# Moving the transposes of the attention probabilities one head closer to their scores, in both attentions of a decoder layer

## The reference, cut to what matters

```
def attention(q, k, v, mask):               # 16 heads of 32 channels
    scores = einsum('bhqd,bhkd->bhqk', q, k) / sqrt(32)
    scores = scores * mask - 10000.0 * (1.0 - mask)
    probs = softmax(scores, axis=-1)
    return einsum('bhqk,bhkd->bhqd', probs, v)
ln_out = layernorm(hidden_states, ln1_s, ln1_b)
q, k, v = split(ln_out @ w_qkv + b_qkv, 3)
x = hidden_states + merge_heads(attention(q, k, v, ltor_mask)) @ w_ao + b_ao
ln_out = layernorm(x, ln2_s, ln2_b)
q = ln_out @ w_q + b_q;  k, v = split(encoder_states @ w_kv + b_kv, 2)
x = x + merge_heads(attention(q, k, v, cross_mask)) @ w_co + b_co
```

## Time and profile before

| | us |
|---|---|
| time, median of 3 runs (4130.07 to 4134.7) | 4130.2 |
| time of the profiled execution | 4134.31 |
| its span | 4132.5 |
| PE busy / DVE busy / ACT busy / POOL busy | 3711.9 / 2993.9 / 2051.7 / 1781.3 |
| first and last L599 of the attentions, from the span's start | 31.1 and 1493.2 |

### The profile page before, as it was taken

How to read it: one execution, slowest core, us unless ns; L and a number is a source line. 1 busy time by engine, 2 the same in 40 slices (tenths; PEclk the granted TensorE clock), 3 DMA queues, 4 the chain that set the end, 5 groups by cost and what they waited for, 6 DMA issues and landing times. The chain is left out here.

```text
span 4132.5 us, 71545 instructions
## 1 busy us (share of the span) xinstructions
PE 3711.9 (90%) x21636; PEld 2875.0 (70%) x21636; DVE 2993.9 (72%) x6732; ACT 2051.7 (50%) x5384; POOL 1781.3 (43%) x1257
## 2 busy tenths in 40 slices
PE   7999999999999969999999679999999999999976
PEld 6777777777777848999999446666666666666633
DVE  6777778888888855665565178888887877888872
ACT  5777777777777755555555213333333333333322
POOL 5444445644444420000000146666566666666652
PEclk9999999999999979999999879999999999999987
DMA  5344344544444441000100300000000000000000
GB/s 147 98 115 107 91 107 115 147 107 118 129 122 111 117 124 52 30 30 31 46 30 26 115 18 14 24 25 24 24 24 25 24 24 24 20 24 18 22 18 15
DMA packets 146675, 256.58 MB, mean 62 GB/s; under 512 B 27248, under 2 KB 32112, under 8 KB 145488
## 3 DMA queue, kind: packets, MB, share of 16 engines
q1 hardware_dynamic: 146512, 254.50, 22.3%
HBM read 107.62 MB, written 33.55 MB: 34 GB/s over the span
## 5 line engine op out<-in xcount | busy, mean ns | idle before, releaser
L432 POOL TENSOR_TENSOR a_prob<-a_prob,a_rsums 128x512 f32<-128x512 f32 x512 | 540.4, 1057 | 780.6 <-DVE a_rsums L610 780.4
L1310 POOL TENSOR_TENSOR c_S<-c_S,c_rT 128x1024 f32<-128x1024 f32 x256 | 558.1, 2180 | 466.4 <-DVE c_S L1588 426.4
L1588 DVE TENSOR_TENSOR_SCAN c_S<-c_wT,c_s,c_vb 128x256 f32<-128x256 f32 x1024 | 709.1, 734 | 46.5 <-issue 4.9
L504 ACT ACTIVATE a_prob<-a_t,a_tmin 128x256 f32<-128x256 f32 x1024 | 512.7, 501 | 366.4 <-DVE a_tmin L603 365.2
L1583 DVE TENSOR_TENSOR c_vb<-c_kT,c_vb 128x512 f32<-128x512 f32 x512 | 352.5, 688 | 293.9 <-PE c_vb L1754 262.2
L599 DVE SCALAR_TENSOR_TENSOR a_ps_s<-a_ps_s,a_mask 128x512 f32<-128x512 f32 x512 | 357.4, 698 | 179.7 <-PE a_ps_s L700 110.6
L603 DVE CUSTOM_DVE_ANT_0 a_t<-a_ps_s,a_mneg 128x256 f32<-128x256 f32 x1024 | 394.2, 422 | 60.1 <-issue 0.7
L1754 PE MATMUL c_vb<-c_vhl,c_spread 128*128 128x512 f32 x512 | 300.7, 597 | 74.5 <-DVE c_S L1588 61.9
L710 PE MATMUL a_ps_t<-w_ident,a_prob 128*128 128x128 f32 x2048 | 323.7, 282 | 27.8 <-ACT a_probT L514 18.1
L971 PE MATMUL b_ps<-b_ln_high,b_w_high 128*128 128x256 f32 x1024 | 291.1, 284 | 15.9 <-DVE b_ln_low L913 15.9
L700 PE MATMUL a_ps_s<-a_stack 96*128 96x256 f32 x1024 | 230.4, 307 | 81.6 <-DMA a_stack<-a_parts_qk 64.6
(11 more groups left out here) (219 smaller groups left out, 9570.6 us busy)
## 6 DMA issues: line engine op xcount, KB each, us to landing
a_stack<-a_parts_qk SPq DMA_DIRECT2D x768, 128.0 KB, 2.4
x<-a_xb SPq DMA_DIRECT2D x32, 512.0 KB, 2.8
a_x_in<-in_x SPq DMA_DIRECT2D x16, 512.0 KB, 3.6
a_xb<-in_x SPq DMA_DIRECT2D x16, 512.0 KB, 3.5
a_x_in<-x SPq DMA_DIRECT2D x16, 512.0 KB, 3.7
a_enc<-in_ctx SPq DMA_DIRECT2D x16, 512.0 KB, 4.4
a_xb<-x SPq DMA_DIRECT2D x16, 512.0 KB, 3.6
b_x_in<-x SPq DMA_DIRECT2D x16, 512.0 KB, 5.1
```

Of the source, the lines that this page charges most:

```text
L432: nc.gpsimd.tensor_tensor(prob[:, h % 4, :, :], prob[:, h % 4, :, :], rsums[:, h, :].unsqueeze(2).to_broadcast([P, TC, T]), ALU.mult).then ...
L504: op = nc.scalar.activation(prob[:, n % 4, tc, :], t[:, n % 2, tc, :], ACT.Exp, bias=tmin[:, n, tc:tc + 1], scale=-1.0, accum_out=psums[:, ...
L1310: nc.gpsimd.tensor_tensor(S[:, n % 4, :, 0:T], S[:, n % 4, :, 0:T], rT[:, par, :, :], ALU.mult).then_inc(z_ready, 1)
L1588: op = nc.vector.tensor_tensor_scan(S[:, n % 4, c, 1:T + 1], wT[:, par, c, :], vb[:, c, :], s0[:, par, c, n:n + 1], ALU.mult, ALU.add)
```

## The change

`LT` becomes 2. With it the transposes of head h stand in step h + 2 of TensorE, behind the scores of head h + 2, and the copy of head h in step h + 2 of ScalarE. Steps 4 and 5 of the list above, on VectorE and GpSimdE, stay where they are.

```
--- before.py
+++ after.py
@@ -126,7 +126,7 @@
     LN_S, LN_B = ("ln1_s", "ln2_s"), ("ln1_b", "ln2_b")
     B_Q, B_K, B_V = ("b_q", "b_qx"), ("b_k", "b_kx"), ("b_v", "b_vx")
     SELF, CROSS = 0, 1
-    LT = 3
+    LT = 2
```

## The result

The changed kernel takes 4356.4 us in the median of 4 runs (4350.97 to 4358.53), the kernel before 4130.1 (median of 4): ratio 1.0544, 95% interval 1.0526 to 1.0562. It is slower, by 226 us; 4336 us were predicted. In the profiled executions the span grows from 4132.5 to 4352.8 us, 220.3 us.

What follows compares the result with a forecast made beforehand. TensorE and VectorE were taken to bound the kernel in turn. Waits of 5.38 us in 32 iterations (172 us) plus 34 us of slower clock made 206 us, on 4130.2 us: 4336 us, range 4240 to 4410 us.

Steps and rivals of the forecast that it cites:

- L(n - 1) + 2.85: Earliest start of step n's transposes, 2.85 us after VectorE's L599 starts in step n - 1, L(n - 1).
- each floor: Least time for two VectorE steps: 3.29 us plus TensorE's time from transposes to next scores.
- Rivals D and E: Whole kernel: D, no measurable change, 4130 us, chance 3%; E, faster by at most 25 us, 4105 us, chance 2%.
- The sum of the waits: Added waiting in one iteration of self-attention, all steps together: 5.38 us; 172 us over 32 iterations.
- 0, 4, 9 and 11: Self-attention steps predicted to lose 1.26, 1.41, 1.36 and 0.79 us, in that order.
- steps 12 to 15: Self-attention steps left out of the sum, as covered by the step before or within 0.2 us.
- Step 2: k3 fill: 0.56 us more, put down to the addition to `a_xb` standing ahead of head 0's multiplication on GpSimdE.
- Cross-attention: Its iterations were taken to lose 5.38 us each too: step 0 nothing, L(0) to L(3) more.
- The clock: One paid half-clock stretch of 1.28 us in every iteration of both attentions: 41 us, less 7 paid already, 34 us.
- A: Whole kernel: waits come as summed, the clock gets no worse; 4302 us, chance 20%.
- rival B: Two slow clock stretches in each iteration, at steps 0 and 9: 4377 us, chance 20%.
- Rival C: Only the long fills of steps 4 and 9 cost: 89 us, 4219 us, chance 10%.

Runs made afterwards that it cites:

- experiment 1: Kernel before, TensorE's and ScalarE's orders kept, but GpSimdE multiplies each head one step later: 4355.2 us, ratio 1.0530.
- 2: Changed kernel, but GpSimdE multiplies only the first 128 queries of each head, the other half left unnormalised: 4244.5 us, ratio 1.0254.
- 8: Changed kernel with TensorE's transposes and ScalarE's copy moved behind the fills, to the end of each step: 4151.0 us, ratio 1.0041.
- experiment 7: Changed kernel with GpSimdE's addition to `a_xb` moved from step 1 to step 6: 4339.4 us, ratio 1.0497.
- experiment 4: Changed kernel plus unread identity matmuls: 2 in step 15, 4 in step 0, 6 in step 8, 6 in some iterations' step 9: 4330.0 us, ratio 1.0472.
- experiment 11: Changed kernel with unread identity matmuls as in experiment 4, but 2 instead of 6 in step 9: 4317.1 us, ratio 1.0442.
- experiment 6: Kernel before, orders kept, but GpSimdE multiplies heads 1 and 6 alone one step later: 4276.4 us, ratio 1.0352.
- 9: Kernel before plus 16 unread identity matmuls ahead of the scores of step 0: 4146.3 us, ratio 1.0031.
- 12: Kernel before plus 7 unread identity matmuls ahead of the scores of step 0, and the addition to `a_xb` in step 6: 4118.5 us, ratio 0.9961.

## Why the prediction was right

- **The mechanism.** Transposes of head n - 2 can't start before L(n - 1) + 2.85, and everything behind them on TensorE's queue waits. The transposes of step 9 start 2.84 us after L(8). Shown further by experiment 1 (the distance alone gives 1.053), by 2 (a shorter multiplication gives back its share of each floor) and by 8 (with nothing long queued behind the wait, 93% of the loss goes). Rivals D and E, that the wait is hidden or that the kernel gains, are out.
- **The sum of the waits.** 5.38 us an iteration of self-attention predicted, 5.73 measured. By steps: 0, 4, 9 and 11 as predicted within 0.12 us (the pairs and triples of steps above; step 11 alone went from 2.33 to 3.17 us, 0.84 against 0.79). The difference is mostly what I had left out in steps 12 to 15, where TensorE also waits: L(13) to L(14) and L(14) to L(15) are 2.47 and 2.50 us, 0.13 and 0.16 longer. Step 2 had the right size and the wrong cause (experiment 7).
- **Cross-attention.** Taken as equal to self-attention, 5.38. In experiment 4, with the clock up, its iterations take 52.14 us against 46.17 before, 5.97 more. 0.35 of it is as in self-attention, and another 0.20 is step 9: L(8) to L(10) is 6.44 us in cross-attention before, not 6.64, so the same floor of 8.00 is short by 1.56 there. What both halves take above 5.38 is most of the 20 us by which the forecast was short: 16 x (0.35 + 0.59) = 15 us.
- **The clock.** 34 us predicted over what was paid before; keeping it up gives back 39 to 42 us in all (experiment 11), of which about 7 were paid before. So 32 to 35 us are new. The places, steps 0 and 9, were right, but the pause named for step 0 was not: the 1.96 us for the restacked q and k are gone, and the idle spells around that stretch are 0.39 us in step 15 and 1.39 us in step 0, both for GpSimdE. The count was not one in each iteration either: self-attention pays one, one and two in turn, at 1.3 to 1.6 us each instead of 1.28, and cross-attention one in every second iteration, at 1.4 us. That too many in one half and too few in the other come out near the 34 us is luck.
- **Rivals A and B.** 4356.4 us lies midway between the forecast and rival B (4377). A, that the clock gets no worse, is out by experiments 4 and 11. B's two paid stretches in each iteration come only in every third iteration of self-attention; the forecast's one in each is nearer, and the rest of the distance is the waits that were summed too low.
- **Rival C**, that only the long fills cost, falls: steps 4 and 9 are 2.8 of 5.7 us, and experiment 6, which has them alone, loses 141 us, with the clock's part, and not 226.
- **Not predicted:** ScalarE's wait for ctx2 and ctx0. The kernel shows it, if one asks for every engine's moved instruction what it must wait for; I had said that the ctx fills wait for copies and had not looked at the copies that wait for ctx fills. It was covered by chance, by the delay of the same steps. One of the signs named ahead failed by it: L(4) to L(5) was to grow by about 1.4 us and grew from 3.95 to 4.33 us, while L(3) to L(4) grew from 2.33 to 3.39. Without that wait, in experiment 1, it is 5.40 us, as said.

## What to carry to other kernels

In an engine that runs its queue in order, what a wait costs depends on how much work is queued behind it that another engine needs, and on the lead that the engine has: two late heads cost 22 us in one place and 141 us in another. Try the instruction that may wait behind the independent work of its step, not ahead of it; here that was 1.0041 against 1.0544. Before shortening a pipeline's lag, take the time at which the operand is ready from the trace and set it against the pace over that many steps, with the largest piece of work in between; and look for the pairs both ways, what the moved instruction waits for and whose buffer it frees or overwrites.

## What the runs showed of the hardware

Idle spells of TensorE cost more than their length here, as the granted clock falls to 0.50 (1.2 GHz) by them: 1.3 to 1.6 us for each stretch that is paid in the changed kernel, 39 to 42 us in all. Not every stretch is paid: in cross-attention the one at step 0 costs nothing. Matmuls whose result nobody reads, put into the spells, kept the clock at 1.00 in nearly all of the attentions (experiments 4, 9, 11 and 12). 7 of them in the pause of 1.96 us cost nothing that shows; 16 of them there took 3.83 us and made the kernel 0.3% slower than before. A matmul of 128x128 in float32 shows as two rows and took 0.24 us.
